# Half-row products in the experts' first layer, and a wait for each GELU ahead of the second

## The reference

```python
logits = (x @ w_g).reshape(N, E)                  # N = 4096 tokens, E = 8 experts
_, topk_idx = jax.lax.top_k(logits, K)            # K = 2
...
xb = jnp.einsum('nec,nd->ecd', sec_mask, xf)      # cap = 1280 places an expert, d = 192
h = jax.nn.gelu(jnp.einsum('ecd,edf->ecf', xb, fc_w) + fc_b, approximate=False)   # f = 768
out = jnp.einsum('ecf,efd->ecd', h, pj_w) + pj_b
y = jnp.einsum('nec,ecd->nd', cb_weight, out)
```

## Time and profile before

| | |
|---|---|
| median of 3 runs | 1075.64 us (1070.26 to 1076.09) |
| profiled execution | 1077.97 us, span 1076.3 us |
| TensorE busy | 944.3 us, 88% |
| ScalarE busy | 676.3 us, 63% |
| VectorE busy | 666.5 us, 62% |
| GpSimd busy | 465.7 us, 43% |
| granted TensorE clock, mean | 0.92 |

### The profile page before, as it was taken

How to read it: one execution, slowest core, us unless ns; L and a number is a source line. 1 busy time by engine, 2 the same in 40 slices (tenths; PEclk the granted TensorE clock), 3 DMA queues, 4 the chain that set the end, 5 groups by cost and what they waited for, 6 DMA issues and landing times.

```text
span 1076.3 us, 22090 instructions
## 1 busy us (share of the span) xinstructions
PE 944.3 (88%) x7210; PEld 723.7 (67%) x7210; DVE 666.5 (62%) x3063; ACT 676.3 (63%) x1446; POOL 465.7 (43%) x508
## 2 busy tenths in 40 slices
PE   2487888999998799999999999567999999999996
PEld 1344655666665566767667766356988888888885
DVE  1576889988987767677767664673344343343332
ACT  2148789979888888778878886264344344344441
POOL 7677666740011001231231122205667666667654
PEclk7668899999999899999989996758999999999999
DMA  7333323321102000101101111226544346454342
GB/s 212 68 61 68 56 53 70 58 34 31 26 12 56 1 2 2 36 2 36 37 1 36 36 36 49 56 52 108 73 83 103 65 100 86 81 103 90 47 49 29
DMA packets 63364, 59.24 MB, mean 55 GB/s; under 512 B 17406, under 2 KB 54304, under 8 KB 63264
## 3 DMA queue, kind: packets, MB, share of 16 engines
q0 software_dynamic: 25344, 27.89, 18.4%
q1 hardware_dynamic: 37728, 29.85, 10.5%
q10 hardware_dynamic: 192, 0.26, 0.1%
HBM read 35.28 MB, written 16.39 MB: 48 GB/s over the span
## 4 chain that ended last, share of the span: by engine, by line
PE 60%; DVE 14%; SPq 7%; ACT 6%; issue 6%; POOL 4%; DMA 3%; POOLq 0%; DVEq 0%; ACTq 0%
PE ps_scores L769 13%; PE ps_ring L761 10%; PE ps_ring L1016 8%; SPq L494 6%; PE ps_ring L769 6%; PE ps_ctx L904 5%; PE ps_scores L1016 4%; PE ps_scores L890 4%; PE ps_scores L887 4%; POOL got L583 3%; DVE probs L1394 2%; DMA k<-k_signed 1%; PE ps_ring L841 1%; PE ps_ring L840 1%; DVE probs L1400 1%
## 5 line engine op out<-in xcount | busy, mean ns | idle before, releaser
L1237 ACT ACTIVATE probs<-ps_scores,fc_bias 128x512 f32<-128x512 f32 (+1 forms) x144 | 88.2, 616 | 148.2 <-PE ps_scores L769 144.7
L643 POOL DMA_INDIRECT out<-z_t,slots_now x80 | 135.4, 1693 | 103.4 <-DVE z_t L1711 84.5
L1105 ACT ACTIVATE prob_t<-ps_ring 128x512 f32<-128x512 f32 x192 | 114.1, 597 | 43.2 <-PE ps_ring L761 42.5
L761 PE MATMUL ps_ring<-ident,probs 128*128 128x128 f32 x768 | 127.9, 293 | 11.7 <-ACT q L1073 6.0
L1130 ACT ACTIVATE probs<-probs,neg_max 128x128 f32<-128x128 f32 x384 | 121.5, 397 | 4.7 <-DVE neg_max L1400 4.7
L1114 ACT ACTIVATE square<-ps_scores 128x512 f32<-128x512 f32 x192 | 104.5, 600 | 26.7 <-PE ps_scores L887 20.0
L1016 PE MATMUL ps_ring<-work,probs 128*128 128x192 f32 x672 | 115.9, 328 | 5.6 <-ACT probs L1237 5.4
L1400 DVE CUSTOM_DVE_ANT_0 probs<-ps_scores,causal 128x128 f32<-128x128 f32 x384 | 88.7, 287 | 50.6 <-PE ps_scores L890 50.4
L1016 PEld LDWEIGHTS ps_ring<-work,probs 128*128 128x128 f32 x672 | 109.2, 190 | 9.4 <-issue 9.4
L761 PEld LDWEIGHTS ps_ring<-ident,probs 128*128 128x128 f32 x768 | 91.9, 149 | 30.9 <-issue 11.0
L769 PE MATMUL ps_scores<-x_hi,fc_hi 128*128 128x512 f32 (+1 forms) x288 | 105.3, 371 | 7.4 <-DVE x_hi L1695 4.8
(11 more groups left out here) (217 smaller groups left out, 2211.7 us busy)
## 6 DMA issues: line engine op xcount, KB each, us to landing
k<-k_signed SPq DMA_DIRECT2D x176, 32.0 KB
work<-pj_w SPq DMA_DIRECT2D x8, 576.0 KB, 4.3
token_in<-xin SPq DMA_DIRECT2D x8, 384.0 KB, 3.1
out<-resid SPq DMA_DIRECT2D x8, 384.0 KB, 4.1
vals<-fc_w SPq DMA_DIRECT2D x8, 384.0 KB, 3.3
vals<-fc_w SPq DMA_DIRECT2D x16, 192.0 KB, 4.0
out<-z_t,slots_now POOLq DMA_INDIRECT x80, 3.6
token_in<-xin SPq DMA_DIRECT2D x8, 128.0 KB, 4.2
```

The lines of the kernel that those rows point to most:

```text
L643: gp.indirect_dma_start(out[:, :], bass.IndirectOffsetOnAxis(slots_now[:, u, 1, t:t + 1], 0), slot_y[:, o, :], None, compute_op=ALU.add).t ...
L761: return pe.transpose(dst, src, ident[0:n, 0:n])
L1105: sc.activation(prob_t[:, s % 2, :, :], src.rearrange("p (h q) -> p h q", h=4), ACT.Exp if p is mag else ACT.Copy).then_inc(ring_free[i], 1)
L1237: sc.activation(hidden[:, c % 2, f_, 0:128 * nt], ps_scores[:, i, 0:128 * nt], ACT.Gelu, bias=fc_bias[:, e, f_:f_ + 1]).then_inc(gelu_done ...
```

## The change

The last of the five products of each group used all 128 rows: high x by low weights in the upper 64 and low x by low weights in the lower 64. In the changed kernel it uses 64 rows: high x by low weights alone. The six groups are taken in pairs. First come the four full products of both groups, then the even group's last product on rows 0 to 63 and the odd group's on rows 64 to 127, into their two banks. For the second of these the high part of x must lie in rows 64 to 127 too: VectorE copies it there, into `x_rest`, which lies over `w_hi` (no longer in use in this stage), right behind the cast to `x_hi`. Both banks of a pair are handed to GELU only after the halves.

In the second layer the three waits ahead of the chunk go, and the first tile waits ahead of each of its six products for that group's GELU.

```diff
+        x_rest = w_hi[:, :, :, :].rearrange("p a b n -> p (a b n)")[:, 0:GROUP * 128]
...
-                for f_ in range(FF_CHUNKS):
-                    i = f_ % FC_RING
-
-                    pe.wait_ge(gelu_done[i], e * 6 + 2 * c + f_ // FC_RING + 1)
-                    col = slice(128 * f_, 128 * f_ + 128)
-                    split_product(ps_scores[:, i, tok], (x_hi[:, 0, tok], x_lo[:, tok], x_hi[:, 1, tok]),
-                                  (fc_hi[:, u, 0, col], fc_lo[:, u, 0, col], fc_hi[:, u, 1, col],
-                                   fc_lo[:, u, 1, col]), False,
-
-                                  begun=pj_used[1 - u] if c == 0 and f_ == 0 else None).then_inc(fc_full[i], 1)
+                top, bottom = slice(0, REST), slice(REST, 128)
+                col = lambda f_: slice(128 * f_, 128 * f_ + 128)
+                for pair in range(FF_CHUNKS // 2):
+                    for f_ in (2 * pair, 2 * pair + 1):
+                        i = f_ % FC_RING
+
+                        pe.wait_ge(gelu_done[i], e * 6 + 2 * c + f_ // FC_RING + 1)
+                        first = pe.matmul(ps_scores[:, i, tok], fc_hi[:, u, 0, col(f_)], x_hi[:, 0, tok],
+                                          start=True, stop=False)
+                        if c == 0 and f_ == 0:
+
+                            first.then_inc(pj_used[1 - u], 1)
+                        for w, x in ((fc_lo[:, u, 0, col(f_)], x_hi[:, 0, tok]),
+                                     (fc_hi[:, u, 0, col(f_)], x_lo[:, tok]),
+                                     (fc_hi[:, u, 1, col(f_)], x_hi[:, 1, tok])):
+                            pe.matmul(ps_scores[:, i, tok], w, x, start=False, stop=False)
+                    for f_, rows_, x in ((2 * pair, top, x_hi[top, 1, tok]), (2 * pair + 1, bottom, x_rest[bottom, tok])):
+                        i = f_ % FC_RING
+                        pe.matmul(ps_scores[:, i, tok], fc_lo[rows_, u, 1, col(f_)], x,
+                                  start=False, stop=True).then_inc(fc_full[i], 1)
...
-                for i in range(FC_RING):
-
-                    pe.wait_ge(gelu_done[i], e * 6 + 2 * c + 3)
                 for t in range(t0, t0 + nt):
...
                     for f_ in range(FF_CHUNKS):
+                        if t == t0:
+
+                            pe.wait_ge(gelu_done[f_ % FC_RING], e * 6 + 2 * c + f_ // FC_RING + 2)
...
                         ve.tensor_copy(x_hi[:, :, tok], x_full[:, :, :]).then_inc(ex_high, 1)
+                        ve.tensor_copy(x_rest[hl, tok], x_full[hl, 1, :])
                         dve.wait_ge(ex_high, e * (CAP_TILES // 2) + m + 1)
```

## The result

The changed kernel takes 1095.72 us (median of 4 runs, 1094.72 to 1099.13) against 1075.87 of the kernel before in the same comparison (4 runs, 1070.26 to 1083.02): a ratio of 1.017 with a 95% interval of 1.013 to 1.022, slower by some 20 us (the ratio is the recorded one; the medians alone give 1.018). The forecast was 1096.

The account below looks back on a forecast made before the run. TensorE, streaming without gaps in the experts' stage, was taken as the bound. Halves +6.6, ring and chain +18, GELU waits -7.5, bias add +2.8, small +0.7 sum to +20.8 us on the median of 1075.64: 1096 us, range 1080 to 1107.

Parts of the forecast that it names:

- The halves: First layer, long chunks: two half products run at once, but each shape switch costs 0.20 us, two a pair; +6.6 us.
- The ring of three banks: Chunk 0's first layer: banks released later, TensorE waits 0.22 us twice; first to last product 4.73 us, not 3.52; +1.2.
- The chain to chunk 1: Chunk 0's last product to chunk 1's first: later GELU, bare load, two copies, +1.05 us; with the ring +18 us overall.
- small terms: Experts' stage: GELU table load holds group 3 longer, +0.4 us; first copy at the very start, +0.3 us.
- The waits for each GELU: Ahead of the second layer in chunks 1 and 2 and at the end: TensorE's idle times for GELU go; -7.5 us.
- The new wait for the bias add: Second layer, chunk 1's fourth tile: its bank comes free later, a wait of about 0.35 us, 8 times; +2.8 us.
- A: Rival: switches of shape in the first layer are free, halves give back 14 us, ring waits grow; 1081 us; chance 0.08.
- C: Rival: TensorE sets the pace everywhere, halves save 14 us, waits 7.5, neither ring nor chain binds; 1054 us; chance 0.04.
- B: Rival: switches cost and the first layer's halves run one after the other; +30 us, 1106 us; chance 0.14.
- D: Rival: only the second layer matters; halves come out even, ring waits vanish, chain +8, waits -7; 1077 us; chance 0.06.

## Why the prediction was right

**The halves, +6.6 us: right.** The steps of 0.32, 0.42 and 0.34 us are those taken from the earlier trace rows. A long chunk's first layer went from 6.86 to 7.05 us from first to last start, and the way out of it from 0.23 to 0.43: 0.39 together, 0.41 forecast; the bare load of the transposes behind it adds 0.06. The halves overlap (both halves on the top rows: +10.9 us), and the switch costs 0.18 us (a half row for each group), against 0.20. Full rows in the same pairs are faster by 12 us, so the halves as such are a loss. One reading behind this term was looser than its result: records of 351 us that cover 89.1 don't alone show that quarters run at once, since the records of products in a row overlap too (30 of 0.39 us cover 7.26). The starts in the same trace do: four quarter-row records begin at 337.281, 337.288, 337.294 and 337.301.

**The ring of three banks, chunk 0: right.** 4.74 us from first to last start against 4.73 forecast, with a wait at groups 3 and 5 of this chunk and none in the long ones.

**The chain to chunk 1: right.** 6.75 us, forecast 6.81; the copy takes 0.29 us, estimated 0.30, and taking it out gives 0.60 a chunk back. With the ring this is +2.21 an expert (11.49 - 9.28), forecast +2.25. Over all experts chunk 0 costs 20.1 instead of 18.7 (18 and the small terms), because of the first expert: its chunk 0 rose by 4.2 us, not 2.2, at a granted clock of 0.50 (see the last section).

**The waits for each GELU, -7.5 us: right in kind, too small.** Measured alone they bring 9.7. The forecast added up the idle times of the earlier trace rows and 0.5 us for the restarts. An idle time is counted from the end of the record before, and that end is modelled: a transpose's record is 0.27 us long, but the next product can start 0.11 after it. Here are the transposes ahead of the second layer of 936.18:

```profile
934.97 0.60 PE L761 MATMUL ps_ring<-ident,xn 128*128 128x128 f32 x4
```

They start 0.11 apart, so the second layer stood 936.18 - 934.97 - 3 x 0.109 = 0.88 us behind the last one, against 0.11 now, and its second record came 0.26 after the first instead of 0.165. That is 0.87 us where the idle time was 0.62, and by the same reading 0.43 us where it was 0.20, in chunk 1. What held it up was the last GELU: in all 24 chunks of the kernel before, the second layer starts 0.23 to 0.26 us after that GELU's end.

**The new wait for the bias add, +2.8 us: right in kind, too small.** It is 0.5 us an expert instead of 0.35 (4.2 / 8, without the copy), since TensorE comes to it earlier by what the quicker start gave. Chunk 1 as a whole changed by +4.3 us, as forecast (8 x (0.41 - 0.22 + 0.35) = 4.3), but that is cancellation: half rows +3.5, waits -3.4, bias add +4.2, where the forecast had +3.3, -1.8 and +2.8.

Sum: +20.8 forecast, +20.6 in the stage, +19.9 in the medians. The small errors (+1.4 in chunk 0, -1.5 in chunk 2, and those inside chunk 1) cancel; the hit to within 1 us is partly luck, also because the executions differ by several us ahead of the stage.

Rivals: A (no price for a switch) and C (faster) fall with the full rows and the half row for each group, B (one after the other) with the halves on the top rows, D with all of them.

## What to carry to other kernels

Before splitting a product over parts of the array, look in the trace for a place where the row count already changes, and read the starts on both sides: here a visit to half rows cost about 0.37 us, and the product it saved 0.233 or 0.117. By these numbers such a visit pays only if more than one pair of half products shares it (an estimate: two pairs of 512 columns would save 0.47 us for 0.37); no run here tries that. When work is paired so that two buffers are handed on at once, redo the sum for the ring behind it and for the longest serial chain that starts from the last of them. Read a gap from start to start, since an idle time leaves out what the modelled end of a record hides. And when a change has two parts, time each alone: here one lost what the other gained and more.

## What the runs showed of the hardware that I had not expected

The first expert begins while the granted clock is low. Its first layer of chunk 0 in the changed kernel, and the same in the kernel before (columns as in the earlier trace rows):

```profile
729.40:737.70 8.30, 7.42 (x30) 6.02 (x30) 0.50 (x3) 2.96 (x5) 3.06 (x5) 0.50 0.88 131
```
```profile
732.70:738.20 5.50, 5.50 (x29) 5.33 (x30) 0.50 (x3) 3.15 (x6) 3.24 (x5) 0.62 0.95 112
```

At 0.50, the lower of the clock's two levels (1.2 GHz), a product of 256 columns starts every 0.21 us instead of 0.117, and the three steps around the halves take 0.35, 0.51 and 0.38 instead of 0.21, 0.31 and 0.22. The first layer took 8.26 us instead of 4.74, and the clock came back to 1.00 at 742.0, 12.6 us after the stage's first product; in the kernel before it came back 4.2 us after it, and that first layer took 5.53. Do the half rows themselves keep the clock low longer? In the profiled executions of the four kernels without them it came back 4 to 9 us after the stage's first product, in the six with them 8 to 13. With one execution each, and the two ranges overlapping, that is a hint and no proof.

Later in the stage the clock fell again in four of the six kernels with half rows and in none of the other four. Each of the six falls to 0.50 came 0.7 to 2.2 us after TensorE had sat idle for 1.2 to 1.3 us, waiting for the GELU behind the table load. But the changed kernel has the same wait twice, the one with full rows waits up to 1.4 us there, and both kept their clock, so the wait alone doesn't decide it, and what does stays open.

Waits that are already satisfied turned out to be free (0.11 us from the last transpose to the second layer, with three of them and with none). What costs is a wait that is not: the second layer started 0.23 to 0.26 us after the end of the GELU it had waited for (all 24 chunks of the kernel before), and its second record then came 0.24 to 0.26 us later instead of 0.165.
